# A graph network on one core: the last nineteen instead of sixteen places of every tile gathered edge by edge, 128 edges at a time, and VectorE's loops over hops and steps written out

## What is computed

```python
deg = maximum(segment_sum(ones, dst), 1); d = deg ** -0.5
h = relu(layernorm(x)); feat = h
for i in range(10):
    agg = segment_sum(feat[src] * (d[dst] * d[src])[:, None], dst)
    feat = (0.9 * agg + 0.1 * h) * reg[i] + (1 - reg[i]) * feat
x = x + feat
e = relu(layernorm(x))
for _ in range(4):
    m = (e @ W_msg.T + b_msg).reshape(3125, 4, 128)
    r = segment_sum(m[src, edge_type], dst)
    e = gru_cell(r, e)
return x + e
```

## Time and profile before

| | us |
|---|---|
| median of three runs | 2250.77 (2250.59 to 2251.88) |
| the profiled execution | 2250.78 |
| its span in the trace | 2248.9 |
| busy in the span: PE, DVE, POOL, ACT | 2064.0, 1346.0, 885.8, 495.3 |

### The profile page before, as it was taken

One profiled execution on the slowest core, in us unless ns is written; L12 is line 12 of the kernel. 1 busy time (PEld: TensorE's weight loads), 2 busy tenths in 40 slices (PEclk: granted clock), 3 DMA queues, 4 the chain that ended last, 5 costly groups with the idle time before them and its releaser, 6 DMA issues.

```text
span 2248.9 us, 42235 instructions
## 1 busy us (share of the span) xinstructions
PE 2064.0 (92%) x15410; PEld 1443.1 (64%) x16017; DVE 1346.0 (60%) x2875; ACT 495.3 (22%) x1130; POOL 885.8 (39%) x1022
## 2 busy tenths in 40 slices
PE   3666665899999999999899999999999999999998
PEld 2333333899989988898655576555765557655576
DVE  8999998777777778786842236422354223553233
ACT  4989887200000000000210002100022000220001
POOL 4978773000000000000058860488604886048870
PEclk9555555899999999999999999999999999999999
DMA  2000000000000000002431111311103111033111
GB/s 83 24 35 35 24 35 36 30 1 2 1 2 2 2 1 2 1 1 91 145 93 42 42 34 40 99 41 42 36 23 113 41 43 37 24 112 70 41 39 31
DMA packets 62730, 89.73 MB, mean 40 GB/s; under 512 B 31953, under 2 KB 48927, under 8 KB 59654
## 3 DMA queue, kind: packets, MB, share of 16 engines
q1 hardware_dynamic: 21185, 54.88, 7.4%
q0 software_dynamic: 38400, 31.28, 6.0%
q10 hardware_dynamic: 2944, 0.93, 0.2%
HBM read 47.48 MB, written 39.05 MB: 38 GB/s over the span
## 4 chain that ended last, share of the span: by engine, by line
PE 75%; DVE 16%; issue 4%; DVEq 3%; ACT 2%; POOL 0%; POOLq 0%; DMA 0%; ACTq 0%
PE ps L912 39%; PE ps L1016 28%; PE ps L895 4%; DVE marks L1218 3%; DVEq L1205 2%; DVE m_full L1688 2%; DVE m_parts L1681 2%; DVE weighed L1223 1%; PE ps L926 1%; DVE dig L1246 1%; DVE big L1248 1%; PE ps L875 1%; PE ps L837 1%; PE ps L1001 1%; DVE hot_pair L1220 1%
## 5 line engine op out<-in xcount | busy, mean ns | idle before, releaser
L508 POOL DMA_INDIRECT big<-messages_by_edge_kind,edge_row x480 | 616.6, 1285 | 1156.7 <-issue 876.2
L912 PE MATMUL ps<-slots,m_parts 125*128 125x436 fp8e4 (+1 forms) x5600 | 960.8, 330 | 4.5 <-DVE m_parts L1681 3.2
L912 PEld LDWEIGHTS ps<-slots,m_parts 125*128 125x128 f16 x5600 | 539.9, 98 | 360.6
L1016 PE MATMUL ps<-parts,big 125*128 125x256 f16 x6125 | 669.0, 273 | 1.1 <-DVEq L1630 1.1
L1016 PEld LDWEIGHTS ps<-parts,big 125*128 125x128 fp8e4 x6125 | 590.7, 98 | 64.1
L1519 DVE TENSOR_SCALAR slots<-big 128x1400 int32<-128x1400 int32 (+1 forms) x224 | 196.5, 920 | 259.5 <-PE ps L912 241.3
L793 PE MATMUL ps<-hot_pair,weighed 125*128 125x228 f16 x1000 | 219.5, 372 | 118.4 <-ACT weighed L621 73.1
L793 PEld LDWEIGHTS ps<-hot_pair,weighed 125*128 125x128 f16 x1000 | 118.0, 124 | 219.8 <-ACT weighed L621 181.3
L621 ACT ACTIVATE weighed<-marks,win_w 125x128 f16<-125x128 f16 x625 | 194.5, 390 | 40.7 <-DVE marks L1218 40.7
L560 ACT ACTIVATE rs<-rs 125x25 f32<-125x25 f32 (+3 forms) x5 | 1.1, 216 | 697.5 <-DVE rs L1088 697.5
L1708 DVE SCALAR_TENSOR_TENSOR gate_r<-ps,over,gate_r 128x436 f32<-128x436 f32 (+2 forms) x32 | 20.0, 624 | 213.6 <-PE ps L895 169.6
(11 more groups left out here) (231 smaller groups left out, 1553.2 us busy)
## 6 DMA issues: line engine op xcount, KB each, us to landing
messages_by_edge_kind<-m_parts SPq DMA_DIRECT2D x20, 1120.0 KB
packed_counts<-packed SPq DMA_DIRECT2D x16, 625.0 KB, 2.9
big<-messages_by_edge_kind,edge_row POOLq DMA_INDIRECT x480
big<-packed_counts SPq DMA_DIRECT2D x4, 1400.0 KB, 6.4
big<-packed_counts SPq DMA_DIRECT2D x3, 1050.0 KB, 5.8
messages_by_edge_kind<-m_parts SPq DMA_DIRECT2D x20, 130.0 KB
hd<-in_x SPq DMA_DIRECT2D x1, 1562.5 KB
x_again<-in_x SPq DMA_DIRECT2D x1, 1562.5 KB
```

The lines of the kernel that those rows point to most:

```text
L508: pool.indirect_dma_start(out=picked[0:CH, r, w, :, :].rearrange("p h f -> p (h f)"), out_offset=None, in_=m_dram[:, :], in_offset=bass.In ...
L912: last = pe.matmul(ps[:, k % 2, 0:SIZES[k] * QD], m_parts[0:Q, a, t, h, :], slots_f8[0:Q, t % 2, 0:SIZES[k], a, 0:QD], start=a == 0 and t ...
L1016: last = pe.matmul(ps[:, n % RING, 0:2 * F], tot_f8[0:Q, c, a, :], both((parts0, parts1)[par], a), start=a == 0, stop=a == TILES - 1)
```

## The change

**More places are picked.** QD falls from 109 to 106, so dense blocks have 424 or 318 columns and the picked turn has 25 x 19 = 475 instead of 400 nodes.

**Other gathers.** The last 127 x 128 = 16,256 edges of the sorted list are gathered, 128 to an indirect DMA, 127 DMAs a step in 26 lots (25 of five, one of two). Each gather adds into a fixed window of 40 picked nodes, whose start `BASES[j]` is a constant; an edge outside its window or ahead of the picked places matches no column. A matmul has 40 columns, adds into the bank at its window, and one matmul with zero weights over all 475 columns clears the bank ahead of a step's first lot. The lots behind (4, 0) move: the last two are added after (6, 0).

**Where the edges come from.** Before, POOL cut the edges of each pair out of the staged tables, and DVE worked out rows and targets in five pieces beside hop 7. Now ACT issues three DMAs behind the first block of counting, which load target, source and type of the last edges with edges across partitions (`"(j p) -> p j"`, single elements of 4 bytes), and DVE does nine operations (`late_edges`) ahead of the last two digit sums. Its test for edges beyond a window enters the flag by one more small matmul. The one-hots are made beside hop 7 in seven pieces (before: hop 8, eight pieces).

**Order.** ACT's and DVE's conversions of the picked sums stand behind the update of block 5's turn instead of ahead of it. The messages' last store is cut in two. POOL makes one more table of numbers and a tile of zeros at the start.

**Loops.** DVE's loop over hops and its loop over steps are written out.

```diff
-QD = 109
+QD = 106
-GW = 15
-PC = 2 * TILES
-PAIRS = (Q - QD) // 2
+GE = 128
+GATHERS = 127
+FIRST_EDGE = E - GATHERS * GE
+PC = 40
+PICKED = TILES * (Q - QD)
+BASES = [min(max(BASE_AT + 31 * (j // BASE_STEP) + 4 * (j % BASE_STEP), 0), PICKED - PC) for j in range(GATHERS)]
+MARKED = 21
-LOTS = PAIRS * GW // LOT
+LOTS = (GATHERS + LOT - 1) // LOT
+LOT_SIZE = [min(LOT, GATHERS - LOT * lot) for lot in range(LOTS)]
-           (3, 0): (11, 12), (3, 1): (13,), (3, 2): (14,), (3, 3): (15,), (4, 0): (16, 17), (4, 1): (18,), (4, 3): (19, 20),
-           (5, 0): (21,), (5, 1): (22,), (5, 2): (23,)}
+LOTS_AT = {... (3, 3): (15,), (4, 0): (16,), (4, 1): (17,), (4, 2): (18,), (4, 3): (19,), (5, 0): (20,), (5, 1): (21,), (5, 2): (22,), (5, 3): (23,), (6, 0): (24, 25)}
-STORED = [(0, 5), (5, 10), (10, 15), (15, 20), (20, 25)]
+STORED = [(0, 5), (5, 10), (10, 15), (15, 20), (20, 23), (23, 25)]
...
-            pool.wait_ge(s_pair, 1)
-            for pair in range(PAIRS):
-                lo = pool.value_load(pair_lo[0:1, pair:pair + 1], min_val=0, max_val=NCH)
...
             block_of(0, 0, BQ, None)
+            with nc.allow_non_contiguous_dma("last edges, 128 at a time"):
+                for to, a in ((late_target, dst), (edge_row[:, :], src), (late_type, edge_type)):
+                    act.dma_start(to, a[FIRST_EDGE:E].rearrange("(j p) -> p j", p=GE)).then_inc(s_late, 16)
...
-                    if u + 1 < TURNS and ORDER[u + 1][0] == "picked":
-                        act.wait_ge(s_got_used[SHELVES - 1], USES * s + USES + 1)
-                        sum_high(picked_sums(0), picked_parts(0, u + 1, 0))
+                    else:
+                        turn, r = divmod(LOTS * (s + 1) - 1, SHELVES)
+                        act.wait_ge(s_got_used[r], turn + 2)
+                        sum_high(picked_sums(0), picked_parts(0, u, 0))
...
+                if lot == 0:
+                    pe.matmul(ps[:, 6, 0:PICKED], zeros[:, :], hot_room[:, 0:PICKED].bitcast(F8), start=True, stop=False, skip_group_check=True)
+                for w in range(LOT_SIZE[lot]):
+                    at = lot * LOT + w
                     for h in range(2):
-                        last = pe.matmul(ps[:, 6, pair * PC:(pair + 1) * PC], picked[0:CH, r, w, h, :], hot_to_f8[0:CH, pair, first + w, :],
-                                         start=first + w == 0 and h == 0, stop=first + w == GW - 1 and h == 1, skip_group_check=True)
+                        last = pe.matmul(ps[:, 6, BASES[at]:BASES[at] + PC], picked[:, r, w, h, :], hot_to_f8[:, at, :],
+                                         start=False, stop=at == GATHERS - 1 and h == 1, skip_group_check=True)
...
+            def late_edges():
+                at = slice(0, GATHERS)
+                rel, base, low, high = late_rel[:, at], late_base[:, at], late_low[:, at], late_high[:, at]
+                dve.wait_ge(s_late, 48)
+                step(TS(base, base, 0.0, float(PICKED - PC), ALU.max, ALU.min))
+                step(TS(rel, late_target, -float(TILES * QD), None, ALU.add))
+                step(TT(win_to[:, :], rel, base, ALU.subtract))
...
+                STT(out=edge_row[:, :], in0=edge_row[:, :], scalar=float(TYPES), in1=late_type, op0=ALU.mult, op1=ALU.add).then_inc(s_rows, 1)
...
             for q in range(BQ * (NB - 1), Q):
                 onehots(q, q % DEPTH, q % WINDOWS)
+            late_edges()
             sum_digits(NB - 2, 0)
...
-                with dve.Fori(0, HOPS // 2 - 2) as i:
-                    steps.loop(i, 2 * (1 + 5 * TILES))
-                    for par in range(2):
-                        hop(2 * i + par, par, TILES * (2 * i + par))
-                steps.done(HOPS // 2 - 2)
-                for h, beside in ((HOPS - 4, scales_beside), (HOPS - 3, edges_beside), (HOPS - 2, targets_beside)):
+                for h in range(HOPS - 4):
+                    hop(h, h % 2, TILES * h)
+                for h, beside in ((HOPS - 4, scales_beside), (HOPS - 3, targets_beside), (HOPS - 2, None)):
                     hop(h, h % 2, TILES * h, beside)
...
-                            if after[0] == "picked":
-                                sum_low(turn + 1, picked_sums(after[1]), picked_parts(after[1], u + 1, 1), picked_parts(after[1], u + 1, 0))
                             unpack(s, i + 1, 1)
...
                     dve.sem_inc(s_emb, 1)
+                    if after and after[0] == "picked":
+                        sum_low(turn + 1, picked_sums(after[1]), picked_parts(after[1], u + 1, 1), picked_parts(after[1], u + 1, 0))
...
-                with dve.Fori(0, STEPS - 1) as s:
-                    steps.loop(s, 4 * TURNS)
-                    gnn_step(s, True)
-                steps.done(STEPS - 1)
-                gnn_step(STEPS - 1, False)
+                for s in range(STEPS):
+                    gnn_step(s, s < STEPS - 1)
```

More of the change, by code:

```diff
@@ L90, with shelf_rows @@
 WD = W - WA
+def shelf_rows(lot):
+    return sum(LOT_SIZE[n % LOTS] for n in range(lot % SHELVES, lot + 1, SHELVES))
 class Chain:
@@ L503, in _ @@
                     for lot in range(LOTS):
-                        r = lot % SHELVES
-                        pool.wait_ge(s_got_used[r], USES * s + lot // SHELVES + 1)
-                        for w in range(LOT):
+                        turn, r = divmod(LOTS * s + lot, SHELVES)
+                        pool.wait_ge(s_got_used[r], turn + 1)
+                        for w in range(LOT_SIZE[lot]):
                             at = lot * LOT + w
                             pool.indirect_dma_start(
-                                out=picked[0:CH, r, w, :, :].rearrange("p h f -> p (h f)"), out_offset=None, in_=m_dram[:, :],
-                                in_offset=bass.IndirectOffsetOnAxis(ap=edge_row[0:CH, at:at + 1], axis=0)).then_inc(s_got[r], 16)
+                                out=picked[:, r, w, :, :].rearrange("p h f -> p (h f)"), out_offset=None, in_=m_dram[:, :],
+                                in_offset=bass.IndirectOffsetOnAxis(ap=edge_row[:, at:at + 1], axis=0)).then_inc(s_got[r], 16)
             with pool.If(over_any > 0):
@@ L920, in picked_rows @@
             def picked_rows(s, lot):
-                r, (pair, first) = lot % SHELVES, divmod(lot * LOT, GW)
-                wait_alone(s_got[r], 16 * LOT * (USES * s + lot // SHELVES + 1))
-                for w in range(LOT):
+                turn, r = divmod(LOTS * s + lot, SHELVES)
+                wait_alone(s_got[r], 16 * shelf_rows(LOTS * s + lot))
+                if lot == 0:
+                    pe.matmul(ps[:, 6, 0:PICKED], zeros[:, :], hot_room[:, 0:PICKED].bitcast(F8), start=True, stop=False, skip_group_check=True)
+                for w in range(LOT_SIZE[lot]):
+                    at = lot * LOT + w
                     for h in range(2):
-                        last = pe.matmul(ps[:, 6, pair * PC:(pair + 1) * PC], picked[0:CH, r, w, h, :], hot_to_f8[0:CH, pair, first + w, :],
-                                         start=first + w == 0 and h == 0, stop=first + w == GW - 1 and h == 1, skip_group_check=True)
+                        last = pe.matmul(ps[:, 6, BASES[at]:BASES[at] + PC], picked[:, r, w, h, :], hot_to_f8[:, at, :],
+                                         start=False, stop=at == GATHERS - 1 and h == 1, skip_group_check=True)
                 last.then_inc(s_got_used[r], 1)
@@ L1175, in _ @@
             dve.wait_ge(s_win_row, 1)
-            begins, ends = (windows[0:1, j * QB + QD:j * QB + Q].rearrange("o (g two) -> o g two", two=2) for j in (0, 2))
-            TT(pair_lo[0:1, :], begins[:, :, 0], begins[:, :, 1], ALU.min)
-            step(TT(pair_hi[0:1, :], ends[:, :, 0], ends[:, :, 1], ALU.max))
-            dve.sem_inc(s_pair, 1)
-            step(TT(pair_span[0:1, :], pair_hi[0:1, :], pair_lo[0:1, :], ALU.subtract))
-            step(dve.tensor_reduce(over1[0:1, 1:2], pair_span[0:1, :], AX.X, ALU.max))
-            step(TS(over1[0:1, 1:2], over1[0:1, 1:2], GW + 0.5, None, ALU.is_gt))
+            step(dve.tensor_reduce(over1[0:1, 1:2], windows[0:1, QD:Q], AX.X, ALU.min))
+            step(TS(over1[0:1, 1:2], over1[0:1, 1:2], (FIRST_EDGE + CH - 1) // CH - 0.5, None, ALU.is_lt))
             dve.sem_inc(s_prep, 1)
@@ L1250, in sum_digits @@
                 dve.sem_inc(s_digits, 1)
+            def late_edges():
[5 more added lines that the diff above has]
+                step(TT(win_to[:, :], rel, base, ALU.subtract))
+                step(TS(low, win_to[:, :], 0.0, None, ALU.is_lt))
+                step(STT(out=low, in0=rel, scalar=0.0, in1=low, op0=ALU.is_ge, op1=ALU.mult))
+                step(STT(out=low, in0=win_to[:, :], scalar=PC - 0.5, in1=low, op0=ALU.is_gt, op1=ALU.add))
+                step(dve.tensor_reduce(over1[:, 2:3], low, AX.X, ALU.add))
+                step(TS(over1[:, 2:3], over1[:, 2:3], -4.0, None, ALU.mult))
```

(3 more changed lines are left out.)

83 lines of the change are left out of this document (26 added, 57 removed).

## The result

The changed kernel takes **2323.3 us** (median of four executions, 2317.2 to 2331.7) against 2251.0 before (2250.6 to 2251.9): a ratio of 1.032, 95% interval 1.028 to 1.036. It is slower, where 2224.7 us and faster were forecast. The profiled execution took 2328.7 us, 77.9 more than that of before.

A forecast was written before the change was run, and what follows sets the result against it. PE, busy 92% of the span, was taken as the bound, except while edges are counted (DVE, ACT). Terms -25.3 + 0.1 - 2.2 + 1.0 + 0.1 + 0.2 = -26.1 from 2250.78 gave 2224.7 us; range 2217 to 2280.

The forecast's parts named there:

- point (2): Steps: POOL's 127 gathers at 1.589 us each finish before PE wants the last lots, covered by 4.4 us.
- C: Rival: POOL's pace decides, 128-row gathers up to 2.4% dearer make last lots late; 2239 at 1.65 us each; chance 0.06.
- ACT gets three DMA issues at about 57 us, 0.51 us each like its earlier ones: Preparation, while edges are counted and ACT is 91% busy: the issues cost 0 to 1.5 us, taken as +1.0.
- rival A: Slower: ACT's loads hold up SP's stores of packed counts, or hold ACT itself at issuing; 2266 to 2354; chance 0.22.
- The dense gathers: Steps: each PE matmul loses 12 or 9 columns at 0.422 ns a column, 60,000 columns in four steps, -25.3 us.
- The gates: Steps: 1,350 columns lost on dense turns and 1,350 gained on the picked turn, same engine and price: 0.
- The picked rows: Steps: 254 matmuls of 40 columns in 26 lots, 5.9 to 7.1 us a step; four steps -2.2 to +2.4, taken as +0.1.
- VectorE's loop over steps: Writing the loop out saves 0.74 us in each of three steps, -2.2 us; block 0 to its third type about 32.9 us.
- The hops: DVE's written-out loop and the marking in seven pieces one hop earlier lie under PE's work: 0.
- The nine operations: Preparation: new DVE operations fit into DVE's 5.03 us wait for ACT's packing, if their loads have landed: 0.
- rival B: Slower: the three loads land after 374 us, needing over 6.5 ns a piece; 2396 at 10 ns; chance 0.03.
- Point (1): Steps: picked sums converted after block 5's turn are ready 6.7 us after its gates, covered by 0.5; uncovered, up to 1 us a step.

The follow-up runs named there:

- before_128: Kernel before, with each of its 120 gathers a step taking 128 rows instead of 125, the extra three read by nothing: 2366.0 us, ratio 1.050.
- loads_sp: Changed kernel with the three element-wise loads issued by SyncE ahead of its first packed store instead of by ScalarE (ACT): 2321.1 us, ratio 1.031.
- rows_125: Changed kernel with gathers of 125 rows, the last three of each 128 edges left out of the sums: 2236.9 us, ratio 0.994.
- whole_125: Changed kernel with 131 gathers of 125 edges instead of 127 of 128, sums whole, and the three loads on SyncE: 2227.3 us, ratio 0.989.
- whole_125_loops: whole_125 with VectorE's two loops (hops and steps) put back: 2243.4 us, ratio 0.997 to the kernel before.
- paced_128_loads_sp: Changed kernel with the loads on SyncE and a 128-element memset holding POOL between its 128-row gathers: 2225.9 us, ratio 0.988.
- loop_or_line: Kernel before plus two stretches ahead of the hops: 600 unused products in a loop, then in straight line, each beside 40 back-to-back gathers; PE stalled in both.
- burst_parts: loop_or_line with other stretches: products beside 40 single-element gathers, then 512-column products beside 40 full-row gathers; PE stalled in the first, after 18.7 us in the second.
- hop_bursts_2: Kernel before plus bursts of 40 unused gathers in the hops: 128 rows held to 1.57 us apart (566 products in 62 us), 112 and 64 rows back to back (PE starved).

## Why the prediction was wrong

**The step that failed is in "New waits", point (2).** It took POOL's gathers as something that could only come too late for PE: it asked what 128 rows cost at worst (2.4% more), and a faster pace had no price. They took 0.94 us instead of 1.21 and came 1.25 us apart instead of 1.51, and that was the loss. No rival had it: C looked at the same engine on the other side. before_128 shows it on the kernel before alone: 115 us. In the changed kernel the steps lost 60.8 us against before instead of gaining 27.

**The second step that failed is "ACT gets three DMA issues at about 57 us, 0.51 us each like its earlier ones".** The price was taken from a load of 512 pieces for loads of 16,256. The first cost 0.38 us, the two behind it 9.47 and 9.85, and the +1.1 of the preparation became 15.7. The second half of rival A had named it ("or they hold ACT itself at issuing"), though its price was worked out for the other half: SyncE's stores were not held, they landed in 2.9 us as before. loads_sp gave the 15 us back to the preparation.

**The dense gathers** were right, and 6 us too small: undisturbed their busy time is 929.9 us (rows_125) against 960.8, 30.9 less instead of 25.3; a column is no dearer, for in rows_125 fifty products of 424 columns take 8.97 us and fifty of 318 take 6.77 (1604.03 to 1610.80), 0.415 ns a column. Each product lost another 1 to 2 ns that its columns don't account for, and no run shows why. **The gates** take 24.2 us a step in both kernels (rows_125, undisturbed): right. **The picked rows**: ten products take 0.28 us as before, so the upper bound held, about 0.5 us a step.

**VectorE's loop over steps**: block 0 takes 33.0 us to its third type in two of the last three steps of whole_125 (1385.12 to 1418.10 in the second step) and 34.7 in the other, where 32.9 was forecast. In that one PE runs some 3 us at the lower of its two clock levels behind a wait of 1.95 us for a message (mean granted clock 0.95 in the stretch, 1.00 in the two others). In the three steps that had been a loop, block 0 is 1.9 us shorter in all; the columns of its first hundred products alone (0.66 us a step) give 2.0, so of the -2.2 nothing is left here. And what the loop would have cost was read from the kernel before; in the changed kernel it costs 16 us (2243.4 against 2227.3; none of the three forecasts of whole_125_loops had it), mostly the 6.5 us at two turns, which in the kernel before took no time. The trace shows what such a turn waits for: behind its branch at 1390.37 VectorE's next instruction begins at 1394.9, and the instruction queue q14 has packets at 1393.1 and 1395.5 (behind the second turn at 1678.5, 1680.9 and 1683.3). In the kernel before q14 has none between 1373.8 and 1581.7. So the turn has code loaded; no gather held that up, as the step's last one was issued at 1351.4. Why the kernel before needs no load there stays open.

**The hops** are 669.6 us in both kernels: right. **The nine operations** run from 385.41 to 388.02 and VectorE still waits 2.51 us for ACT after them: right. **The loads** landed 11.6, 20.5 and 21.8 us after their issue, so rival B was far off, and so was the price of 3.6 ns a piece: the last took 1.34 ns a piece, everything included. The Trainium skill (DMA: Bandwidth & Descriptors, Rules for kernel authors) has a strided last dimension as one descriptor per element; the page's queue q10 agrees, with 51,760 packets where the kernel before had 2,944; 48,768 of the difference are the elements. Its 10.5 ns a packet (section Bandwidth) does not fit these landings. **Point (1)** held: PE waited 0.5 us once ahead of the gates. In point (2), POOL's start 35.5 us into the step is 1.2 less than its own rows give (1138.67 + 5.4 - 1107.41 = 36.7); it started after 34.4 (1123.15 to 1157.55), so the slip cost nothing.

With both losses out, paced_128_loads_sp (2225.9) and whole_125 (2227.3) end within 3 us of the 2224.7 of the forecast. That is partly luck: in whole_125 the dense gathers gave 5.7 us more than forecast (929.8 us busy), and late lots (4.8) and the missing gain of the loop (2.2) took more than that back.

**What stays open** is how a gather holds PE's instructions. Excluded are the fetching of code (loop_or_line), the gathered bytes and the rows (burst_parts, hop_bursts_2), the packets on the queue (128 rows 1.35 us apart leave 32 a gather and cost PE more than 125 rows 1.50 us apart, which leave 80), and PE's operands, which in loop_or_line and burst_parts are one constant tile. In every run each gather adds 16 to a semaphore when it lands; that was not varied. The Trainium skill (SBUF — State Buffer, Who interferes with whom) says that DMA has ports of its own and never contends with an engine; that the bytes don't matter agrees, but TensorE was held beside DMAs all the same. If the rule holds, these ports are not what the two share; no run here shows what it is. The Trainium skill (NOTIFIC — the notification-queue block, Overflow: three behaviours, one of which stalls the engine) says that the records of instructions pass a block whose inner queues hold back the engine when they fill. By that rule the stall could belong to the recording of the executions, since each one timed here was recorded; no run here shows it either way, nor whether an execution that nothing records has the loss.

## What to carry to other kernels

An engine off the critical path that becomes faster is a change to every other engine: ask what its new pace does to them, and try that one thing on the old kernel alone, as before_128 did. The price of a DMA issue is not that of the last one seen: here it rose from 0.38 to 9.47 us when the issue ahead of it on the same queue had 16,256 pieces, so long element-wise loads belong on an engine with nothing behind them. And when PE stands with no releaser in straight code, look at what else began some 6 to 20 us earlier, not at the moment of the stall.

## What the hardware showed that was not expected

- A gather of 64, 112 or 128 rows takes 0.90 to 0.95 us on POOL, one of 125 rows 1.20 to 1.21: more rows can be cheaper. The first three leave 32 packets on the queue, 125 rows leave 80.
- 40 gathers 1.2 to 1.35 us apart bring PE from 37 products in 4 us down to 2 or 3 (5 at 1.35 us); at 1.57 us they cost it next to nothing. It begins after some 120 to 250 of PE's instructions and ends 2 to 9 us after the last gather.
- An element-wise load of 16,256 pieces holds the next DMA issue of its engine for 9.5 us on ACT, and for up to 28.7 us on SyncE early in the kernel.
- The turn of a loop on VectorE costs nothing where the instruction queue has nothing to load (1395.78 in the kernel before) and 6.5 us where it loads code (whole_125_loops).
